# A two-layer graph kernel: inputs of a step prepared further ahead, and the order of all five engines rewritten

## The reference, cut to what matters

```
h = relu(layernorm(x))
x = x + L0(h)                  # max over channels of relu(adj @ h + b), one number for each node
h = relu(layernorm(x))
q, k, v = split(h @ w_qkv)     # 8 heads of 32
s = where(adj == 0, -inf, q @ k.T * 32**-0.5)
o = softmax(s) @ v @ w_proj + b_proj
out = x + o + layernorm(o) * gamma + beta
```

## Time and profile before

| | us |
|---|---|
| three timed runs | 1016.46, 1011.68, 1025.72 |
| median | 1016.46 |
| profiled execution | 1012.41 |
| its span, first to last instruction | 1010.7 |
| PE busy with matmuls | 817.2 (81%) |
| DVE busy | 645.9 (64%) |
| ACT busy | 489.5 (48%) |
| POOL busy | 429.1 (42%) |
| DMA engines, mean share | from 0.6 to 0.7 in most slices |
| chain that ended last: PE / DMA | 63% / 17% |

### The profile page before, as it was taken

One profiled execution on the slowest core, in us unless ns is written; L12 is line 12 of the kernel. 1 busy time (PEld: TensorE's weight loads), 2 busy tenths in 40 slices (PEclk: granted clock), 3 DMA queues, 4 the chain that ended last, 5 costly groups with the idle time before them and its releaser, 6 DMA issues.

```text
span 1010.7 us, 31246 instructions
## 1 busy us (share of the span) xinstructions
PE 817.2 (81%) x11241; PEld 536.8 (53%) x11241; DVE 645.9 (64%) x1552; ACT 489.5 (48%) x1192; POOL 429.1 (42%) x853
## 2 busy tenths in 40 slices
PE   1578998788789888888987888798888889997862
PEld 0235665455556555555655555565555566654641
DVE  3554776666667666766765666686576677775653
ACT  3334555454455545545554444555454455553441
POOL 5411554344454434434544343454334445542343
PEclk9788998899999989989998998999899899998885
DMA  4466564667655676676556767555677755655313
GB/s 122 91 143 140 119 130 107 133 137 142 127 99 134 126 128 133 142 148 109 116 127 121 131 137 147 100 125 127 118 138 134 129 122 132 131 117 95 81 23 42
DMA packets 168295, 121.34 MB, mean 120 GB/s; under 512 B 84720, under 2 KB 167408, under 8 KB 167664
## 3 DMA queue, kind: packets, MB, share of 16 engines
q1 hardware_dynamic: 67328, 69.72, 27.2%
q10 hardware_dynamic: 83952, 33.04, 20.8%
q0 software_dynamic: 16896, 16.78, 11.2%
HBM read 35.06 MB, written 33.55 MB: 68 GB/s over the span
## 4 chain that ended last, share of the span: by engine, by line
PE 63%; DMA 17%; issue 9%; DVE 3%; SPq 3%; ACT 3%; POOL 2%; ACTq 1%; DVEq 0%; POOLq 0%
PE a_ps L319 20%; DMA hT<-h_lo 15%; PE sum_ps L446 8%; PE sc_ps L396 6%; PE pv_ps L416 6%; PE sum_ps L419 4%; PE a_ps L304 4%; PE sc_ps L368 4%; PE sc_ps L344 4%; SPq L273 2%; PE a_ps L332 2%; PE sum_ps L443 2%; ACT o_sb L590 1%; PE pv_ps L431 1%; ACTq L533 1%
## 5 line engine op out<-in xcount | busy, mean ns | idle before, releaser
L319 PE MATMUL a_ps<-hT,w_hi 128*128 128x512 f16 x512 | 170.6, 467 | 96.0 <-DMA hT<-h_lo 94.6
L844 POOL TENSOR_TENSOR oT_lo<-oT,oT_hi 128x256 f16<-128x256 f32 x128 | 84.6, 670 | 297.4 <-ACT oT_hi L584 297.3
L673 DVE TENSOR_REDUCE smax<-sc_ps 128x4 f32<-128x512 f32 x256 | 163.7, 681 | 51.7 <-PE sc_ps L368 51.6
L561 ACT ACTIVATE pairs<-a_ps 128x512 f16<-128x512 f32 x128 | 77.8, 608 | 231.1 <-PE a_ps L319 231.1
L665 DVE TENSOR_TENSOR pairs<-a_ps,pairs 128x512 f16<-128x512 f32 x128 | 87.3, 682 | 125.8 <-ACT pairs L561 125.8
L319 PEld LDWEIGHTS a_ps<-hT,w_hi 128*128 128x128 f16 x512 | 53.6, 115 | 168.2 <-issue 113.5
L838 POOL TENSOR_TENSOR h_lo<-h_sb,h_hi 128x256 f16<-128x256 f32 x128 | 89.1, 698 | 116.9 <-ACT h_hi L524 116.5
L571 ACT ACTIVATE p_sb<-sc_ps 128x512 f32<-128x512 f32 x256 | 137.1, 610 | 1.0 <-PE sc_ps L396 0.9
L578 ACT ACTIVATE pv_sb<-pv_ps 128x256 f32<-128x256 f32 x128 | 50.5, 394 | 146.2 <-issue 97.4
L416 PE MATMUL pv_ps<-p_sb,v_sb 128*32 128x128 f32 x2048 | 107.2, 278 | 6.1 <-ACT pv_sb L578 2.6
L723 DVE SCALAR_TENSOR_TENSOR t_sb<-o_sb,mv,w_sb 128x256 f32<-128x256 f32 x128 | 70.1, 586 | 60.9 <-POOL w_sb L869 60.9
(11 more groups left out here) (105 smaller groups left out, 1545.0 us busy)
## 6 DMA issues: line engine op xcount, KB each, us to landing
stack<-pairs SPq DMA_DIRECT2D x768, 64.0 KB, 2.0
out<-in_x SPq DMA_DIRECT2D x32, 512.0 KB, 4.2
out<-y_sb POOLq DMA_DIRECT2D x32, 512.0 KB, 8.4
x_sb<-in_x ACTq DMA_DIRECT2D x31, 512.0 KB, 3.6
stack<-crow SPq DMA_DIRECT2D x64, 8.0 KB, 1.9
w_sb<-in_L_gnn_w_qkv SPq DMA_DIRECT2D x1, 768.0 KB, 7.1
x_sb<-in_x SPq DMA_DIRECT2D x1, 512.0 KB, 3.7
hT<-h_hi ACTq DMA_TRANSPOSE x32, 6.3
```

What stands on the lines that cost most here:

```text
L319: mm = nc.tensor.matmul(a_ps[c % 2][:].rearrange("p (b n) -> p b n", b=G), w[:, dc, col:col + P], hT[:, par, part, :, dc], start=(k == 0), ...
L673: nc.vector.tensor_reduce(smax[:, HC * j:HC * (j + 1), b], sc_ps[u % SC_SLOTS][:], AX.X, ALU.max).then_inc(smax_ready, 1)
L844: nc.gpsimd.tensor_tensor(oT_lo[:, b], oT[:, b], oT_hi[:, b], ALU.subtract).then_inc(olo_ready, 1)
```

## The change

The load of x moves from two steps ahead of use to three (`load_x(t + 3)`), the LayerNorm numbers from one step ahead to two (`stats_x(t + 2)`, `invert_std_x(t + 2)`), and h, which was made and transposed late in the step before its use, is now made at the start of that step and transposed in its middle. rstd1, shift1, h_hi and h_lo get three buffers, so that they wait for the readers of step t-2 and not of step t. The helper `pipeline` passes one more flag (norm). All five ORDER lists are new. The matmuls, activations, vector instructions and DMAs of a full step stay the same in number and shape.

The diff, cut to what the text below speaks of:

```diff
-        shift1 = sb("shift1", [P, G])
+        shift1 = sb("shift1", [P, SLOTS, G])
         ve1 = sb("ve1", [P, G])
-        rstd1 = sb("rstd1", [P, G])
+        rstd1 = sb("rstd1", [P, SLOTS, G])
         h_sb = sb("h_sb", [P, G, D])
-        h_hi = sb("h_hi", [P, G, D], F16)
-        h_lo = sb("h_lo", [P, G, D], F16)
+        h_hi = sb("h_hi", [P, SLOTS, G, D], F16)
+        h_lo = sb("h_lo", [P, SLOTS, G, D], F16)
...
-                step(t, t % SLOTS, t < STEPS, 1 <= t <= STEPS, 2 <= t <= STEPS + 1, t >= 3, t + 1 < STEPS, t + 2 < STEPS)
+                step(t, t % SLOTS, t < STEPS, 1 <= t <= STEPS, 2 <= t <= STEPS + 1, t >= 3, t + 1 < STEPS, t + 2 < STEPS,
+                     t + 3 < STEPS)
...
-            ORDER = ("Q0 M0 C0 Q1").split()
+            ORDER = ("M0 Q0 C0 Q1").split()
...
-            ORDER = ("K0 S0 S1 S2 R0 S3 Q0 Q1 R1 N0 E0 E1 E2 L0 R2 E3 O0 R3 K1 S4 O1 L1 S5 S6 O2 S7 O3 Q2 M0 N1 E4 E5 "
-                     "P0 P1 E6 E7 P2 P3 Q3 P4 P5 V0 P6 P7 V1").split()
+            ORDER = ("K0 S0 S1 R0 S2 Q0 S3 R1 Q1 R2 N0 E0 E1 O0 E2 E3 L0 R3 O1 K1 S4 S5 S6 S7 O2 L1 O3 N1 E4 M0 P0 P1 "
+                     "Q2 P2 P3 E5 E6 Q3 E7 P4 P5 V0 P6 P7 V1").split()
...
+            def h_high(t, par, b):
                 act.wait_ge(h_ready, G * t + b + 1)
                 if b == 0:
-                    wait(act, a_psum, 2 * t)
-                    wait(act, hT_in, 32 * t)
-                nc.scalar.activation(h_hi[:, b], h_sb[:, b], ACT.Copy).then_inc(hhi_ready, 1)
+                    wait(act, a_psum, 2 * (t - 2))
+                    wait(act, hT_in, 32 * (t - 2))
+                nc.scalar.activation(h_hi[:, par, b], h_sb[:, b], ACT.Copy).then_inc(hhi_ready, 1)
...
+                act.wait_ge(x_loaded, 16 * t)
                 nc.scalar.dma_start(x_sb[:, par], xg[t]).then_inc(x_loaded, 16)
...
-            ORDER = ("Q0 C0 X0 Q1 C1 E0 E1 E2 E3 C2 O0 C3 O1 R0 R1 H0 O2 R2 O3 H1 M0 H2 R3 A0 Q2 E4 E5 E6 A1 H3 E7 Q3 "
-                     "A2 T0 A3 V0 L0 V1").split()
+            ORDER = ("R0 H0 C0 Q0 C1 Q1 E0 E1 C2 O0 E2 E3 O1 R1 C3 H1 R2 O2 H2 R3 O3 M0 H3 E4 A0 T0 Q2 A1 E5 E6 Q3 E7 "
+                     "A2 L0 X0 V0 A3 V1").split()
...
-                        load_x(t + 2, (k + 2) % SLOTS)
+                        load_x(t + 3, k)
...
             load_x(1, 1)
             for b in range(G):
                 rectify(0, 0, b)
             for b in range(G):
-                h_high(0, b)
+                h_high(0, 0, b)
+            load_x(2, 2)
...
-            ORDER = ("I0 I1 I2 S0 O0 S1 S2 S3 Q0 O1 X0 X1 O2 O3 Q1 L0 B0 S4 S5 B1 B2 S6 S7 B3 G0 M0 L1 F0 Q2 F1 Q3 F2 "
+            ORDER = ("I0 I1 I2 S0 S1 O0 S2 O1 S3 Q0 O2 Q1 X0 O3 B0 L0 B1 S4 S5 S6 S7 B2 B3 X1 M0 G0 L1 F0 F1 Q2 Q3 F2 "
...
-                            stats_x(t + 1, (k + 1) % SLOTS)
+                            stats_x(t + 2, (k + 2) % SLOTS)
                         else:
-                            aggregate_x(t + 1)
+                            aggregate_x(t + 2)
...
             stats_x(0, 0)
             aggregate_x(0)
             split_core()
+            stats_x(1, 1)
+            aggregate_x(1)
...
-            ORDER = ("C0 C1 X0 C2 C3 H0 H1 N0 H2 W0 W1 W2 H3 W3 K0 D0").split()
+            ORDER = ("C0 C1 H0 C2 C3 H1 H2 H3 N0 W0 W1 K0 W2 W3 X0 D0").split()
...
+                        invert_std_x(t + 2, (k + 2) % SLOTS)
```

More of the change, by code:

```diff
@@ L228, in pipeline @@
                 for k in range(SLOTS):
-                    step(t + k, (k + 1) % SLOTS, True, True, True, True, True, True)
+                    step(t + k, (k + 1) % SLOTS, True, True, True, True, True, True, True)
             for t in range(STEPS - SLOTS - 1, STEPS + SLOTS):
@@ L273, in stack_heads, with step @@
                         nc.sync.dma_start(dst.rearrange("p s b n -> p s (b n)"), src).then_inc(stacked[j], 16)
-            ORDER = ("Q0 M0 C0 Q1").split()
-            def step(t, k, a, sc, e, d, prep, load):
+            ORDER = ("M0 Q0 C0 Q1").split()
+            def step(t, k, a, sc, e, d, prep, norm, load):
                 for what in ORDER:
@@ L757, in step @@
                         qk_low(t, i)
-                    elif kind == "X" and prep:
+                    elif kind == "X" and norm:
                         if i == 0:
-                            stats_x(t + 1, (k + 1) % SLOTS)
+                            stats_x(t + 2, (k + 2) % SLOTS)
                         else:
-                            aggregate_x(t + 1)
+                            aggregate_x(t + 2)
             def split_core():
@@ L819, in carry_waits, with invert_std_x @@
                 nc.gpsimd.tensor_tensor(pool_cell[:, cell:cell + 1], pool_cell[:, 0:1], pool_cell[:, 0:1], ALU.add)
-            def invert_std_x(t):
+            def invert_std_x(t, par):
                 pool.wait_ge(mv1_ready, G * (t + 1))
-                wait(pool, h_ready, G * t)
+                wait(pool, h_ready, G * (t - 2))
                 carry_waits(1)
@@ L885, in step @@
                         o_low(t - 3, i)
-                    elif kind == "X" and prep:
-                        invert_std_x(t + 1)
+                    elif kind == "X" and norm:
+                        invert_std_x(t + 2, (k + 2) % SLOTS)
                     elif kind == "H" and prep:
-                        h_low(t + 1, i)
+                        h_low(t + 1, (k + 1) % SLOTS, i)
                     elif kind == "N" and d:
```

32 lines of the change are left out of this document (16 added, 16 removed).

## The result

Four runs of the changed kernel: 979.39, 963.08, 975.86 and 971.01 us, median **973.43 us**. The kernel before had 1015.54 us over four runs. The ratio is 0.9537, 95% interval 0.942 to 0.9653: faster; it leaves out the run of 979.39 us, which lies over 1.5% above the fastest. The profiled execution is that run, with a span of 977.6 us; where the time went is read from its span against the 1010.7 us of before.

The account below looks back on a forecast made before the run. SP's ring was taken to set the step: a mean of 28.6 us over 28 intervals, 0.7 less than before, -19 us, and +6 us at the start. 1012.4 - 19 + 6 = 999 us, range 948 to 1050 us.

Parts of the forecast that it names:

- list of signs: hT wait under 8 us; stack waits 30 to 50 us; P0's crow wait about 1.1 us; SP gapless; clock 0.95+.
- The ring, 28.0 us, through set 1 and S4: On SP, M0 through crow, both stack sets, landing, S4 to next M0: 28.0 us a step, ends 25.1 and 30.0.
- A: The forecast itself: SP's ring takes most of what the transposes give back; 999 us (985 to 1020), chance 0.55.
- Why the sets would be long: On SP, two sets of stack DMAs sum to 19.7 us, the one beside the transposes stretched by 2 us.
- The transposes' time in hand, 1.6 us: Transposes land at M0 + 12.8, the next Q0 on PE stands 14.4 us behind M0: 1.6 us in hand.
- PE's own step, 25.7 us: PE's step without SP's ring: 23.4 us, plus 1.1 for P0 behind M0, plus 1.2 for A1 late.
- The 1.2 us that A1 was to come late: ACT, held 4.39 us by the transposes, ends A1 after PE needs it for P4: +1.2 us a step.
- rival B: SP keeps up: sets take 16.8 us, ring 25.1 us, PE's 25.7 us sets the step; 951 us, chance 0.20.
- The start, +6 us, and the drain, 0: Second step took 19.3 us, the ring allows no less than 25.1: +6 us; the end keeps its chain: 0.
- The jump: At a loop turn's end PE's step gains 3.95 us and 0.85 us of low clock: 30.5 us in 7 steps.
- Rival C: Slower than before: waits for the sets cost clock from S4 to M0, up to 2.5 us a step; 1052 us, chance 0.20.
- Rival D: Transposes land 2.5 us later, so Q0 on PE still waits; bites only with rival B; 970 us, chance 0.05.

Follow-up runs that it names:

- Experiment 1: The changed kernel with SP's list alone put back from M0 Q0 C0 Q1 to Q0 M0 C0 Q1; 902.4 us, ratio 0.8898.
- Experiment 8: The changed kernel without the transposes of groups 3 to 31 and the waits for them; 970.35 us, ratio 0.9598.
- experiment 9: The changed kernel with the load of x moved in ACT's list from behind A2 to behind Q0; 1005.09 us, ratio 0.9857.
- experiment 12: The changed kernel with SP's old list, all 35 steps written out, and the load of x moved behind Q0 on ACT; 931.55 us, ratio 0.9067.
- experiment 5: The changed kernel, new SP list kept, with the transposes put back behind A2 in ACT's list; 1020.65 us, ratio 1.0206.
- experiment 7: The kernel before with SP's list alone changed to M0 Q0 C0 Q1; 1102.56 us, ratio 1.0856.

## Why the prediction was right, and where it was not

**The mechanism held.** The wait for hT went, the waits for the stack and for crow came, SP's list ran without gaps and had 6.0 us free behind it, the clock was 0.95. Each stood in the list of signs. Experiment 1 shows it by removal: the swap on SP takes back 71 us of what the rest of the change brings, 973 for 902. Forecast were 999 us and a chance of 0.44 for faster; measured are 973.4, inside the range. That the number is not further off is in part luck, since several terms missed in opposite ways. In the profiled execution, 20 us under the forecast, the steps gave 18 us more than I had and the start 9, and the end took 6 back. The terms:

- **The ring, 28.0 us, through set 1 and S4.** It closes at S0 in most steps, at S4 in some; the mean over the 21 intervals without a jump is 27.5, and 29.4 over the 7 with one, where I had 30.5. For both sets I took the 19.7 us of the earlier trace rows; they are 8.90 and 9.12 on average, 18.0. For the landing I took the 2.0 us median of the earlier trace rows. It holds for the last DMA of set 1 in 7 of the 8 steps in which S4 waits; for the last of set 0 it is 3.6 to 5.3 us in the 14 steps in which the chain goes through it. The median is that of all 768, and the ring goes through one with a load, a store and a copy around it. A term of a ring has to be read at its place. Third, I had no clock in the ring under A: S0 to M0 is 11.9 us at a clock of 1.00 and 13.1 on average.
- **Why the sets would be long.** I put the 2 us by which a set was longer in the earlier trace rows down to the transposes beside it. Experiment 8 doesn't show that: without them set 0 averages 8.59 us for 8.90, and the time is the same (970 for 973). Their own landing did stay long, a median of 5.1 us for the first, and the 2.0 us for both that I worked out by the Trainium skill, DMA: Bandwidth & Descriptors, section Latency and other measured facts, was an estimate that no row here reaches: one alone took 2.9 us at the least. But the clean sets that I drew from it (2 x 8.82) were closer than my own 19.7.
- **The transposes' time in hand, 1.6 us.** In the step shown the second is issued at M0 + 3.9, and at the median of 5.4 us it lands at M0 + 9.3, 6.3 us before the next Q0 (523.78). I had taken the 8.62 us of one step. In that sum 0.9 and 0.4, for P0, P1 and A0, stand twice; what belongs there, the issue of the first transpose, happens to be as long, 1.3 us.
- **PE's own step, 25.7 us.** It is 24.2 on average and 23.8 in a quiet step (experiment 1). P0's 1.1 us are there, 0.96 in the step shown. The 1.2 us that A1 was to come late are 0.3: 6.4 us of wait for it from 300 to 900 us in experiment 1. ACT is held 2.9 us and not 4.39: that was one step, and the medians of the two issues were 1.86 and 1.72 us before and are 1.32 and 1.40 now, beside set 0 and not set 1. In a quiet step 23.8 - 1.0 = 22.8 us are left for the base that I put at 23.4. The condition of **rival B**, SP keeps up, did not come true in the changed kernel; experiment 1 makes it true, and B's price was too high: 951 us where it takes 902.
- **The start, +6 us, and the drain, 0.** They were -2.9 and +6.0. Together 3 and not 6 us; the written-out steps were not read closely enough to place it.
- **The jump.** That a turn's end costs PE 4.8 us over a plain step was in my sum, and only as a part hidden by the ring. In the changed kernel a jump adds 29.4 - 27.5 = 1.9 us, since SP's ring covers most of it; once the ring is gone it adds 4.7 (experiment 1).

**Rival C** did not come at its price, but its mechanism is there, at S0 and not at S4. C had 2.5 us in every step; measured are 13.1 - 11.9 = 1.2 us a step without a jump, S4's waits included, and a mean clock of 0.95, not 0.92. I had taken from the earlier trace rows that a wait over 1.62 us costs the clock. S0 waits 2.84 us at 522.98 and the clock to the next M0 is 1.00; it waits 2.92 us at 494.64 and the clock is 0.87. In experiment 9 a wait of 2.92 us before S4 is followed by sixteen matmuls in 1.85 us, where 1.07 is full speed; in experiment 12 one of 2.49 us at the same place is followed by 1.07 us. The length of one wait does not decide it; what does is not settled by these runs. **Rival D** did not come either: no wait for hT behind the start.

Left open: how the late landing of set 0 divides between load, store and copy. The load was moved (experiment 9); store and copy alone were not tried. Nor is it only a matter of what is issued beside it: in the step with M0 at 784.7 load and store go out as in the others, at 792.9 and 795.5, and S0 comes at M0 + 12.8 with a wait of 0.77 us. What is different there is not known. Also open is why the clock is lower in experiment 5, and what of a jump's 4.7 us is on engines other than PE.

## What to carry to other kernels

A list that is executed in order makes a ring as soon as a wait stands ahead of work that does not need it, and the ring's length is the sum of everything queued behind that wait; before moving a waiting entry up, add up the ring, and then the one through the next consumer too. Read each term at its place in the ring and not as a median over all of its kind: here the landing was 3.8 us where the median said 2.0. A wait inside a ring can cost more than its length, because the matmuls behind it may run at the lower clock. When a ring is near the bound, don't place a large transfer by looking at one consumer; moved away from set 0, the load of x hit set 1.

## What the runs showed of the hardware that I had not expected

- A 64 KB DMA of the stack landed in 2.0 to 3.1 us before a 512 KB load was issued, in 3.5 to 4.2 us behind it (experiment 8, one step), in 3.6 to 5.3 us at the end of set 0 in 14 steps of the changed kernel, with a 512 KB load, store and copy issued near it, and in 6.2 and 7.3 us in experiment 7.
- Two stretches with the same 157 matmuls, behind waits of 2.92 and 2.84 us, took 13.5 us at a granted clock of 0.87 and 11.9 us at 1.00.
- Moving one 512 KB load in each step by some 20 us cost 32 us in one kernel (experiment 9) and 57 us or more in another (experiment 12); nothing is added or removed.
- A loop's jump back made its step 4.7 us longer with 7 jumps in the run and 6.8 us with 3. In experiment 1 PE's own gap there is up to 3.4 us, named "issue". A straight program of 35 steps had no such gap and ran at a clock of 1.00 from 112 to 800 us.
- Two DMA transposes held ACT's list for 2.7 us on average in the changed kernel; and leaving out 58 of them changed the time of this kernel by 3 us, less than can be told apart.
